# Turning tiles with 64-row transposes on both row halves of the tensor engine, in a two-layer transformer kernel with windowed attention

## What is computed

```python
for i in range(DEPTH):                                   # 6
    x = attn_layer(shift_tokens(x), Wqkv[i], ...) + x    # 16 heads of 64, windows of 32
    x = ffn_layer(shift_tokens(x), ...) + x              # 128 -> 2 x 341 -> 128, exact GELU

def attn_layer(x, Wqkv, qs, ksc, Wo):
    q, k, v = split(x @ Wqkv)                 # each (b, 16, n, 64)
    q, k = l2norm(q) * qs, l2norm(k) * ksc    # then a rotation by position, scaled
    sim = q . k over the own and the previous window of 32, times 8, masked
    out = softmax(sim) @ v
    return out @ Wo
```

## Time and profile before

| | us |
|---|---|
| median of three runs | 2197.93 (2195.68 to 2202.28) |
| span of the profiled execution | 2182.5 |
| TensorE busy | 2005.7 (92%) |
| VectorE busy | 1809.4 (83%) |
| ScalarE busy | 1579.9 (72%) |
| GpSimd busy | 1167.3 (53%) |

### The profile page before, as it was taken

The page is one execution under the profiler, slowest core; times in us unless marked ns, Lnnn a source line. Parts: engine busy times, 40 slices in busy tenths (PEclk is TensorE's granted clock), DMA queues, the critical chain, the costliest instruction groups (busy, mean ns, idle before and its releaser), DMA issues.

```text
span 2182.5 us, 82607 instructions
## 1 busy us (share of the span) xinstructions
PE 2005.7 (92%) x34395; PEld 1457.7 (67%) x34395; DVE 1809.4 (83%) x3751; ACT 1579.9 (72%) x3031; POOL 1167.3 (53%) x1413
## 2 busy tenths in 40 slices
PE   6888899987699999999999999999999999999997
PEld 4666654455577776777777777777767777677775
DVE  7888765678798998888988888988888988888884
ACT  4777753365577887787877788777787878887773
POOL 1112110000577676666776667666667767667761
PEclk9999999998899999999999999999999999999999
DMA  4000001000122232222322223322232322332221
GB/s 114 1 2 2 2 31 59 30 1 30 52 72 68 61 105 69 68 63 71 90 72 75 66 58 95 81 68 66 70 87 71 87 58 58 102 82 62 75 59 40
DMA packets 98196, 132.18 MB, mean 61 GB/s; under 512 B 27900, under 2 KB 42882, under 8 KB 97826
## 3 DMA queue, kind: packets, MB, share of 16 engines
q1 hardware_dynamic: 97826, 126.90, 22.0%
HBM read 28.20 MB, written 1.11 MB: 13 GB/s over the span
## 4 chain that ended last, share of the span: by engine, by line
PE 72%; DVE 13%; issue 6%; ACT 6%; POOL 1%; SPq 1%; DMA 0%; DVEq 0%; POOLq 0%; ACTq 0%
PE oo L586 21%; PE pj L586 19%; PE tr L589 14%; PE sc L586 13%; ACT arena L1924 3%; PE tr L586 2%; DVE arena L1729 2%; DVE xn L1318 2%; DVE arena L1486 1%; PE oo L589 1%; DVE arena L1731 1%; DVE arena L1750 1%; DVE arena L1752 1%; PE sc L589 1%; ACT sc L1924 1%
## 5 line engine op out<-in xcount | busy, mean ns | idle before, releaser
L2345 POOL TENSOR_TENSOR arena<-arena 128x1024 f32<-128x1024 f32 x192 | 456.9, 2380 | 336.9 <-DVE arena L1731 336.9
L1924 ACT ACTIVATE arena<-tr 128x512 f32<-128x512 f32 (+2 forms) x874 | 460.8, 570 | 111.9 <-PE tr L589 109.7
L1924 ACT ACTIVATE arena<-pj 128x512 f32<-128x512 f32 x576 | 341.7, 599 | 189.5 <-PE pj L586 150.4
L589 PE MATMUL tr<-ident,arena 128*128 128x128 f32 x2882 | 413.3, 279 | 25.3 <-DMA beta<-in_L_attn_betas 9.8
L1924 ACT ACTIVATE arena<-arena 128x16 f32<-128x16 f32 (+6 forms) x808 | 362.3, 454 | 98.7 <-DVE arena L1486 74.0
L589 PEld LDWEIGHTS tr<-ident,arena 128*128 128x128 f32 x2882 | 330.6, 141 | 93.4 <-issue 34.5
L2363 POOL TENSOR_TENSOR arena<-arena 128x1024 f32<-128x1024 f32 x192 | 366.7, 1910 | 23.2 <-POOL arena L2356 0.9
L1729 DVE TENSOR_TENSOR arena<-pj,rtab 128x512 f32<-128x512 f32 x384 | 259.8, 677 | 24.8 <-ACT arena L1924 23.4
L586 PE MATMUL oo<-slab,arena 64*32 64x64 f32 (+1 forms) x12416 | 232.1, 228 | 41.0 <-issue 26.4
L1731 DVE TENSOR_TENSOR arena<-pj,rtab 128x512 f32<-128x512 f32 x384 | 261.4, 681 | 0.0
L1737 DVE TENSOR_REDUCE arena<-arena 128x8 f32<-128x512 f32 x384 | 255.6, 677 | 0.0
(11 more groups left out here) (289 smaller groups left out, 3802.5 us busy)
## 6 DMA issues: line engine op xcount, KB each, us to landing
slab<-arena SPq DMA_DIRECT2D x576, 128.0 KB, 2.4
slab<-arena SPq DMA_DIRECT2D x336, 64.0 KB, 2.0
wqkv<-in_L_ffn_Wqkv SPq DMA_DIRECT2D x18, 512.0 KB, 4.2
arena<-gate_mem SPq DMA_DIRECT2D x24, 256.0 KB, 4.3
wo<-in_L_ffn_Wo SPq DMA_DIRECT2D x6, 512.0 KB, 4.2
w<-in_L_ffn_W SPq DMA_DIRECT2D x6, 341.0 KB
YT<-in_L_attn_x SPq DMA_DIRECT2D x4, 256.0 KB, 3.5
arena<-in_L_ffn_W SPq DMA_DIRECT2D x1, 1024.0 KB
```

The source lines that it names most:

```text
L589: return nc.tensor.transpose(o, i, ident[0:i.shape[0], 0:i.shape[0]])
L1924: return nc.scalar.activation(o, i, f, **k)
L2345: p_.tensor_tensor(r_, r_, rb[:, k, :], ALU.add).then_inc(sum_ok, 1)
```

## The change

TensorE: a turn is now sixteen transposes of 64 rows by 128 columns. For each of the 8 pairs of heads, rows 0 to 63 go to bank 0 and rows 64 to 127 to bank 1, one after the other. So both banks are written from the start of the turn to its end, both copies are released by the turn's last two transposes, and each turn waits once, for both copies of the turn before it. `window_scores` and `values` wait for both copies of their turn ahead of their first half. In the slot, `probs` stands ahead of projection 2, and projections 2 and 3 follow each other.

ScalarE: each copy takes one bank, all 8 pairs by 64 rows, into places 128 apart. Query copy 1 stands ahead of GELU 0, and both copies of the probabilities stand ahead of square 2.

```diff
-def turn(g, t, j):
-
-    pe.wait_ge(qk_rdy, g * 2 + j // 2 + 1)
-    for u in range(4):
-        pr = 4 * (j % 2) + u
-        last = tp(tr[:, j % 2, u * P:(u + 1) * P], ra[:, t % 2, j // 2, pr * P:(pr + 1) * P])
-    last.then_inc(qk_tr, 1)
-
-def turn_probs(g, j):
-
-    for u in range(4):
-        pr = 4 * j + u
-        last = tp(tr[:, j, u * P:(u + 1) * P], Ex[:, 2 * pr:2 * pr + 2, :])
-    last.then_inc(e_tr, 1)
-
-def turn_out(g, j):
+def turn_rows(rows, done):
+
+    for pr in range(PAIRS):
+        for u in range(2):
+            r = slice(u * DL, (u + 1) * DL)
+            last = nc.tensor.transpose(tr[:, u, pr * DL:(pr + 1) * DL], rows(r, pr), ident[r, r])
+            if pr == PAIRS - 1:
+                last.then_inc(done, 1)
+
+def turn(g, t, k):
+
+    pe.wait_ge(qk_rdy, g * 2 + k + 1)
+    turn_rows(lambda r, pr: ra[r, t % 2, k, pr * P:(pr + 1) * P], qk_tr)
+
+def turn_probs():
+
+    turn_rows(lambda r, pr: Ex[r, 2 * pr:2 * pr + 2, :], e_tr)
+
+def turn_out(g):
 
     pe.wait_ge(on_ok, g + 1)
-    for u in range(4):
-        pr = 4 * j + u
-        last = tp(tr[:, j, u * P:(u + 1) * P], On[:, pr * P:(pr + 1) * P])
-    last.then_inc(on_tr, 1)
+    turn_rows(lambda r, pr: On[r, pr * P:(pr + 1) * P], on_tr)
...
-    pe.wait_ge(qk_cp, g * 4 + 3 + i)
     if i == 0:
+        pe.wait_ge(qk_cp, g * 4 + 4)
         pe.wait_ge(masked, g + 1)
...
-    pe.wait_ge(pt_cp, g * 2 + 1 + i)
+    pe.wait_ge(pt_cp, g * 2 + 2)
...
     def turn_q():
-        for j in range(2):
-            if g >= 3:
-                pe.wait_ge(o_cp, (g - 3) * 2 + j + 1)
-            elif g == 2:
-                pe.wait_ge(qk_cp, 3 + j)
-            turn(g - 1, t - 1, j)
+        if g >= 3:
+            pe.wait_ge(o_cp, (g - 2) * 2)
+        elif g == 2:
+            pe.wait_ge(qk_cp, 4)
+        turn(g - 1, t - 1, 0)
 
     def turn_k():
-        for j in range(2):
-            if d_:
-                pe.wait_ge(pt_cp, (g - 2) * 2 + j + 1)
-            else:
-                pe.wait_ge(qk_cp, (g - 1) * 4 + j + 1)
-            turn(g - 1, t - 1, 2 + j)
+        if d_:
+            pe.wait_ge(pt_cp, (g - 1) * 2)
+        else:
+            pe.wait_ge(qk_cp, (g - 1) * 4 + 2)
+        turn(g - 1, t - 1, 1)
 
     def probs():
         pe.wait_ge(e_exp, g - 1)
-        for j in range(2):
-            if c_:
-                pe.wait_ge(qk_cp, (g - 1) * 4 + j + 1)
-            else:
-                pe.wait_ge(o_cp, (g - 3) * 2 + j + 1)
-            turn_probs(g - 2, j)
+        if c_:
+            pe.wait_ge(qk_cp, (g - 1) * 4 + 2)
+        else:
+            pe.wait_ge(o_cp, (g - 2) * 2)
+        turn_probs()
...
     def out_():
-        for j in range(2):
-            if c_:
-                pe.wait_ge(qk_cp, (g - 1) * 4 + j + 3)
-            else:
-                pe.wait_ge(pt_cp, (g - 2) * 2 + j + 1)
-            if t == 0 and m2 is not None:
-                pe.wait_ge(ff_ev, m2 * FFC + 2)
-            if t == 3 and j == 0 and m1 is not None:
-                pe.wait_ge(lnb_out, m1 + 1)
-            turn_out(g - 2, j)
+        if c_:
+            pe.wait_ge(qk_cp, g * 4)
+        else:
+            pe.wait_ge(pt_cp, (g - 1) * 2)
+        if t == 0 and m2 is not None:
+            pe.wait_ge(ff_ev, m2 * FFC + 2)
+        if t == 3 and m1 is not None:
+            pe.wait_ge(lnb_out, m1 + 1)
+        turn_out(g - 2)
...
+    if d_:
+        probs()
     if new:
         if b == 0 and t == 0:
             pe.wait_ge(wl_ok[1], l + 1)
         project(g, t, 2)
         if g == 0:
             crossing(g, 1)
-    if d_:
-        probs()
-    if new:
         project(g, t, 3)
         crossing(g, 2)
...
-    for j in range(2):
-        pe.wait_ge(o_cp, (TZ - 2) * 2 + j + 1)
-        turn(TZ, T - 1, j)
+    pe.wait_ge(o_cp, (TZ - 1) * 2)
+    turn(TZ, T - 1, 0)
...
-    src = tr[:, j % 2].rearrange("p (a b) -> p a b", b=P)
-    pr = slice(4 * (j % 2), 4 * (j % 2) + 4)
-    dst = qT[:, pr, :] if j < 2 else kT[:, pr, WIN + t * P:WIN + (t + 1) * P]
+    src = tr[:, j % 2].rearrange("p (a b) -> p a b", b=DL)
+    at = j % 2 * DL
+    dst = qT[:, :, at:at + DL] if j < 2 else kT[:, :, WIN + t * P + at:WIN + t * P + at + DL]
...
-    act(PT[:, 4 * j:4 * j + 4, :], tr[:, j].rearrange("p (a b) -> p a b", b=P), ACT.Copy
+    act(PT[:, :, j * DL:(j + 1) * DL], tr[:, j].rearrange("p (a b) -> p a b", b=DL), ACT.Copy
         ).then_inc(pt_cp, 1)
...
-    act(oT[:, 4 * j:4 * j + 4, t * P:(t + 1) * P], tr[:, j].rearrange("p (a b) -> p a b", b=P),
+    act(oT[:, :, t * P + j * DL:t * P + (j + 1) * DL], tr[:, j].rearrange("p (a b) -> p a b", b=DL),
         ACT.Copy).then_inc(o_cp, 1)
...
     if c_:
         take_qk_part(g - 1, (t - 1) % T, 0)
+    if c_:
+        take_qk_part(g - 1, (t - 1) % T, 1)
     if t == 0 and m2 is not None:
         gelu(m2, 0, FFB[0])
         log_exp_tables()
-    if c_:
-        take_qk_part(g - 1, (t - 1) % T, 1)
+    if d_:
+        take_probs(g2, 0)
+        take_probs(g2, 1)
     if new:
         ac.wait_ge(ss_ok, g * 4 + 1)
         square(g, 2)
...
     if layer_end:
         table(g + 1, l + 1, 0)
-    if d_:
-        take_probs(g2, 0)
     if s_.ahead is not None and t == 1:
         if l > 0 or b == B - 1:
             ac.wait_ge(y_ff, n + 1 - B + 2)
...
-    if d_:
-        take_probs(g2, 1)
     if new:
         ac.wait_ge(ss_ok, g * 4 + 2)
         square(g, 3)
...
```

More of the change, by code:

```diff
@@ L1252, in drain @@
                 pe.wait_ge(e_exp, TA + 1)
-                for j in range(2):
-                    pe.wait_ge(qk_cp, TZ * 4 + j + 1)
-                    turn_probs(TA, j)
+                pe.wait_ge(qk_cp, TZ * 4 + 2)
+                turn_probs()
                 values(NB - 1, TA, T - 2, 0)
-                for j in range(2):
-                    pe.wait_ge(pt_cp, TA * 2 + j + 1)
-                    turn(TZ, T - 1, 2 + j)
+                pe.wait_ge(pt_cp, TA * 2 + 2)
+                turn(TZ, T - 1, 1)
                 values(NB - 1, TA, T - 2, 1)
@@ L1262, in drain @@
                 window_scores(TZ, T - 1, 1)
-                for j in range(2):
-                    pe.wait_ge(qk_cp, TZ * 4 + j + 3)
-                    turn_out(TA, j)
+                pe.wait_ge(qk_cp, TZ * 4 + 4)
+                turn_out(TA)
                 final(0)
@@ L1268, in drain @@
                 pe.wait_ge(e_exp, TZ + 1)
-                for j in range(2):
-                    pe.wait_ge(o_cp, TA * 2 + j + 1)
-                    turn_probs(TZ, j)
+                pe.wait_ge(o_cp, TA * 2 + 2)
+                turn_probs()
                 pe.wait_ge(f_cp, 2)
@@ L1276, in drain @@
                 ff_up(MY, 1, LAST_FF[MY][1])
-                for j in range(2):
-                    pe.wait_ge(pt_cp, TZ * 2 + j + 1)
-                    turn_out(TZ, j)
+                pe.wait_ge(pt_cp, TZ * 2 + 2)
+                turn_out(TZ)
                 last_out_project(0)
```

## The result

The change makes the kernel slower: 2231.26 us (median of 4 runs, 2227.19 to 2240.87) against 2199.45 for the kernel before on the same chip, a ratio of 1.0154 with a 95% interval of 1.0129 to 1.0179. That is 32 us more, where 11 us less was forecast: inside the stated range of 2140 to 2250 us, but on the other side of the kernel before. Of the rivals, the fourth (the new waits are dearer, 2216 us) comes nearest.

What follows compares the result with a forecast made beforehand. TensorE was taken to set the pace, with little slack on VectorE and ScalarE. Gains of 7 us (slots) and 6 (late issue) less 2.5 (layer ends) gave 10.5, from 2197.9 to about 2187 us; range 2140 to 2250.

Steps and rivals of the forecast that it cites:

- the length of a turn: Every TensorE turn: sixteen 64-row transposes take 0.45 us from first to last start, against 0.81 before.
- rival 1: Every turn: the halves don't run side by side, 0.82 us to the last start; 2267 us, chance 0.13.
- Rival 2: Every turn: load and stream of one half don't overlap, so a turn takes 1.56 us; 2425 us, chance 0.03.
- what a turn saves net: TensorE's turns, less 0.10 us per change of shape: 0.95 us a slot in t = 0 and 1, 1.25 otherwise.
- t = 0: First of a block's four tile slots: only TensorE binds, so its whole saving is kept, gain 1.0 us.
- t = 2: Third tile slot: ScalarE idles 0.7 us and the second key copy adds 0.5, scores 1.2 later; gain -1.0 us.
- t = 1: Second tile slot: query turn waits 0.5 us more for the second output copy, shorter turns repay it; gain 0.1.
- the 37.5 us of late issue: TensorE's waits that nothing in the profile explains, taken as late instructions; forecast to fall by 6 us.
- t = 3: Fourth tile slot: VectorE sets it; the probabilities' turn waits for query copies, replacing the key projection's wait; gain 0.
- TensorE's 4.4: Saving in us a block from the shorter turns, 106 us in all, if TensorE alone decided.
- Rival 4: New waits are dearer: t = 1 loses 0.5 us unpaid, t = 3 0.7 of idle time; 2216 us, chance 0.17.
- Rival 3: t = 0 to 2: ScalarE's chain does not bind, TensorE keeps its gain of 3.2 us a block; 2121, chance 0.12.

Runs made afterwards that it cites:

- release_late: Kernel before with the probabilities' turn and copies in the new order, 128-row turns, each step waiting for its own bank's copy, both copies released at turn's end: ratio 1.0045.
- wait_both: Kernel before with the new order, 128-row turns filling and releasing bank 0 then bank 1, but waiting for both copies of the turn before: ratio 1.0166.
- t0_rows: Kernel before with the new order in t = 0, 1 and 3, plus 64-row turns waiting for both copies in t = 0 only: ratio 0.9921.
- the order alone: Kernel before with the probabilities' turn ahead of projection 2 and ScalarE's copies in the new order, turns still 128 rows in two steps: ratio 0.9967.
- both_copies: Changed kernel's order, waits for both copies and release at the end, but with eight 128-row transposes a turn: ratio 1.0272 to the kernel before.
- rows_only: Changed kernel with the probabilities' turn back between projections 2 and 3 and its copies behind square 2; 64-row turns stay: ratio 1.0184 to the kernel before.
- mixed: Changed kernel with the probabilities' turn ahead of projection 2 only in t = 0 and 1, between projections 2 and 3 otherwise: ratio 1.0133 to the kernel before.

## Why the prediction was wrong

**Right: the length of a turn.** From first to last start it takes 0.486 us, a step of 0.0324 against the 0.030 that I took, and the bound was 0.033 for rival 1; turn to next product is 0.64 where 0.605 was worked out. So the halves run side by side and rivals 1 and 2 were wrong. Rival 2 was worked out from a sentence of the Trainium skill, in TensorE: Matmul & The Clock Gate, Part 3, by which a load overlaps products in flight only when its row group differs. The trace goes against that sentence here too, and not only at full height: within one half a transpose starts every 0.065 us, while its load lasts 0.142.

**Wrong: what a turn saves net.** TensorE's sum for t = 0 was 0.95 us: 0.25 for the output turn, 0.15 each for the query turn and the probabilities' turn, 0.4 for the key turn. In undisturbed slots it is 0.19 (last score to the second product behind the turn, 1.31 before and 1.12 after), 0.04, 0.03 and 0.38, together 0.64. The query turn of t = 0, in a slot before and in one after:

```profile
1277.78 1.88 PE L586 MATMUL oo<-hT,w 128*128 128x512 f32 x4
1279.50 1.04 PE L589 MATMUL tr<-ident,arena 128*128 128x128 f32 x8
1280.38 3.62 PE L586 MATMUL sc<-arena,wo 128*128 128x256 f32 x16
1283.64 0.47 PE L586 MATMUL sc<-xs_hi,wq_hi 128*128 128x256 f32 x1
```

```profile
1300.78 1.88 PE L586 MATMUL oo<-hT,w 128*128 128x512 f32 x4
1302.59 0.71 PE L1009 MATMUL tr<-ident,arena 64*128 64x64 f32 x16
1303.23 3.72 PE L586 MATMUL sc<-arena,wo 128*128 128x256 f32 x16
1306.60 0.47 PE L586 MATMUL sc<-xs_hi,wq_hi 128*128 128x256 f32 x1
```

The way in costs 0.09 (1.81 against 1.72), as forecast. On the way out the next product starts 0.15 us after the last transpose, 0.05 of it the transpose itself, also as forecast; but the group behind the turn then takes 0.10 longer (first to first start 3.37 against 3.26), which the sum did not have. From end to end it is 5.82 against 5.86. The change of shape was mis-sized, and with it a third of the saving in t = 0 was never there.

**Near: TensorE's busy time.** Down by 42 us instead of 100; but the 22 stretches at half clock lie over work that would have taken half of their 78 us, 39 us, and without them it would be 81, an estimate.

**Right: t = 2.** Every point of the chain came within 0.3 us of where it was put: probabilities' turn 1.98 us after the query turn (1.9 from the text's numbers), copies done at 3.8 (3.7), `xcur` at 6.1 (5.9), mask at 7.2 (6.9), scores at 8.35 (8.1). The slot lost 1.23 in the median, against 1.0. `release_late` and `wait_both` show the two halves of it as argued: 0.46 for the idle ScalarE, 0.80 for the second copies.

**Wrong: t = 1, "the shorter turns give that back, gain 0.1".** The wait came as written (the query turn starts 2.10 us after the first read of the scores instead of 1.62, 0.48 late), and the slot lost 0.48 in the median. The shorter turns did give time back: by the second half of the values TensorE is ahead (9.18 against 9.34 in the median), and in the median its first scores start level (11.06 against 11.03). But the second half of the values takes 1.10 us in the mean from first to last start instead of 0.79, and the first half of the scores 0.94 instead of 0.74, held up in 14 of 23 slots instead of 7. The time was given back and lost again to late instructions, and the mean of the slot is 0.61 longer.

**Wrong: t = 0, "gain 1.0".** It was 0.06 in the median and 0.42 in the mean. A third of the 0.95 is the net saving above: TensorE gained 0.62 up to projection 4. Of that, 0.2 in the mean were lost in the first half of the scores, as `t0_rows` shows again by itself. The step that failed beside the price is the term "of the 37.5 us of late issue ... I take 6 us less": by the trace late issue did not shrink. Ahead of values and scores it was 31.9 us before and is 41.8 after. I took it to fall, had the 64 additional instructions in view and gave them no price.

**Wrong: t = 3, "gain 0".** In slots with a full clock the values do start where they were forecast (7.19 us after the first read of the scores in the slot shown, against 6.92 in the median of before), and such slots have a median of 13.72. But in most of them the clock falls and costs about 1.5 us, and the median of all is 15.19 against 14.48. The prediction moved the probabilities' turn to the end of a gap that it had measured, and never asked what the clock does behind it. `wait_both`, with one such stretch in the whole stage, also loses 0.64 here over the order alone, so with 128-row turns the waits cost too.

**The sum.** The forecast was a gain of 0.1 us a block from TensorE's 4.4. In the traces the four slots gave +0.42, -0.61, -1.31 and -0.68 in the mean instead of +1.0, +0.1, -1.0 and 0. Measured by the ratios, about 2195 us each: order -7, waits for both copies +44, release at the end +23, 64-row transposes -25, together +34. The transposes' 106 us came down to 25: part of it was not there, part lies where TensorE then waits for ScalarE or for its own instructions, and the low clock took some. Rival 4 comes nearest, t = 1 unpaid and the probabilities' idle time in t = 3, at 29 us over the forecast; 44 were needed, and in t = 3 of the changed kernel much of the loss is the clock, which it did not have. Its chance of 0.17 was too low: the text had itself worked out that only 0.1 of 4.4 us would be left, and a difference so small between two large terms could not carry 48% for faster. Rival 3 (ScalarE's chain doesn't bind) is dead: TensorE's waits for ScalarE in turns and scores are 111 us.

## What to carry to other kernels

When two buffers are handed over one by one, each half's release and each half's wait are worth a term of their own: here giving up both cost 3.1%, nearly three times the 1.1% that the shorter turns brought. Before an engine's work is made cheaper, find what it waits for next. Price a change of shape from the product before it to the end of the group behind it, and hold the engine's unexplained waits against the packets of the instruction queue: time saved just ahead of such a wait can be lost in it. And when an empty gap of TensorE is gathered into one place, look at the granted clock behind it.

## What was not expected of the hardware

The granted clock can fall to half behind a gap of some 2 us inside a stage in which TensorE is busy 89% of the time. Whether the length of the gap or the kind of transposes decides is not shown: `both_copies`, with 128-row transposes, has a gap of 1.88 us at the same place where the change has 2.11, and one low stretch instead of 22; `rows_only` and `mixed`, with 64-row transposes and a typical wait of 0.26 us there, have 6 and 8, most of them behind waits of 1.1 to 2.0 us at other places.

A wait of TensorE that the view calls "issue" ends, in nine of ten groups of short products that are held up, 1.20 to 1.55 us after a packet of the instruction queue has landed (91% of 53 groups in the kernel after, against 7% of the groups that are not held up).
